# Transformer chain on one core: slots of all steps placed anew, first batch's start reordered, Newton's steps for 1/norm moved from VectorE to GpSimdE

## The chip, the cores and the metric

The kernel runs on one core of a Trainium2 chip. The core has TensorE (matmuls; PE in the profile, its weight loads are PEld), VectorE (DVE), ScalarE (ACT), GpSimdE (POOL) and SyncE (SP), which here issues all the DMAs. The engines run beside each other, each its own program in order, and meet through semaphores. The metric is the time of one execution on the device, in microseconds (us); lower is better.

## The reference

The input x has 16 batches of 512 tokens with 128 channels. Four blocks are added to it in turn, each on the layernorm of x:

```
x = x + attn_a(layernorm(x))      # latent attention, 16 heads, causal, softmax
x = x + ffn(layernorm(x))         # sigmoid(xr W_r) * (relu(xk W_k)^2 W_v), x mixed with the token before
x = x + attn_b(layernorm(x))      # q and k normalised to length 1 per head, causal, softmax of 8 * q.k
x = x + ffn(layernorm(x))
```

The step of attn_b that the change touches is

```
q, k = (t / max(sqrt(sum(t * t)), 1e-12) for t in (q, k))     # per token and head, 8 channels
```

## The kernel before

**The work of a batch.** All 512 tokens of a batch are worked on at once, as 4 tiles of 128. A batch passes these stages (methods of `Stages`, one version for each engine):

- `prepare_front`: layernorm "1" (statistics on DVE, `rstd` on POOL, `xn` on DVE, transposed by PE, evicted as `xnT` by ACT), then `project`: queries and keys by two matmuls (L611), each result split in three bf16 parts, part 0 by ACT (L874), part 1 by DVE (L1045, L1048), part 2 by POOL (L1296). SP writes the parts to DRAM (`scratch`) in the three pieces of `STACK` (L1433).
- `restack`: SP reads them back with the products of parts stacked along the contraction (`stack_qa`, `stack_ka`, L1453).
- `row_maxima` and `max_rows`: all scores of attention a once for their maxima (PE L636, DVE L1074, in two groups of pairs), which are turned and written into rows of `stack_qa` by four small DMAs (`mturned`, L1472).
- `attend a`: scores again (L705), `exp` on ACT (L923, `prob`), weighted sums (L722, `acc`); `middle_front`: residual and the first feed-forward block.
- `middle_back`: layernorm "3", `project_qk` (L777), sums of squares `ssum` (DVE L1167), `rsqrt`, `turn_qk` (L1199 multiplies by `rnorm`, PE L795 transposes, split as above), then `restack` and `attend b`; `finish`: output projection and the second feed-forward block, `store`.

**rsqrt.** 1/sqrt(`ssum`) for 128 x 128 numbers is made on DVE from an integer seed (two operations, L1178 and L1180) by three steps of Newton, each three operations on DVE (L1184, L1187, L1189), eleven in all. The POOL version of `rsqrt` is empty.

**What sets the order.** `halves` lists the 32 attention halves (a and b of each batch, the a half three batches ahead); each has 36 slots. `stages_of` gives each yield of a stage a slot, by the table `PLANS` relative to its half: a class `None` for most batches, and classes for batches 0, 1, 2, -2 and -1. `turns` sorts all yields by slot and runs them through the generators of each engine, so the table sets the order in which every engine's instructions stand. `Places` runs the same order first and gives out the PSUM banks (`pool0` to `pool3`), each free when its former user's reader is done. `setup` is a stage too, with three yields: identity and constants; the five products of weights for the first projection (PE L581, L585; ACT L841, L838) with POOL's `ones_rows` and masks; the other products and POOL's clearing of `vals`. PE leaves such a yield only when all its products have been evicted.

**In the steady part** DVE's maxima for the next batch, ACT's exponentials and PE's matmuls of two halves are interleaved. Three two-bank tiles of PSUM are shared by the maxima (freed by DVE) and the scores (freed by ACT).

Of the kernel before, what the change touches and what calls it, by code (L numbers as in the profile page):

```python
# [6 lines left out]
ALU, ACT, AX = mybir.AluOpType, mybir.ActivationFunctionType, mybir.AxisListType  # L7
# [21 lines left out]
SLOTS = 36  # L29
# [19 lines left out]
        "half_norm_b": [27],  # L49
        "finish": [34, 35, 39, 42, 45, 49, 54, 54, 56, 57, 63, 68],  # L50
    },
    0: {
        "load": [-159],
        "prepare_front": [-138, -125, -114, -113, -109],
        "restack_a": [-73, -68],
        "row_maxima0": [-63.8, -62.2, -53.8, -50.8, -45.2, -45.2, -42.8, -42.2, -36],
        "max_rows0": [-24, -23],
        "row_maxima1": [-31, -30.2, -20, -16.2, -14.8, -10.8, -6.2, -1.8, -1.8],
        "max_rows1": [1, 6],
        "values_a": [-38, -32],  # L60
        "half_norm": [19],
        "middle_front": [39, 41, 47, 51, 54, 57, 61, 63, 69, 71],
        "restack_b": [95, 98],
        "middle_back": [72, 75, 78, 81, 81, 82, 83, 86, 89, 90, 92],
        "values_b": [-42, -30],
        "half_norm_b": [27],
# [4 lines left out]
        "prepare_front": [-62, -59, -53, -48, -46],  # L71
        "restack_a": [-42, -37],
        "row_maxima0": [-29, -28, -28, -27, -26, -25, -22, -18, -18],
        "max_rows0": [-17, -15],
        "row_maxima1": [-14, -14, -10, -8, -7, -6, -5, -5, -4],
        "max_rows1": [0, 6],
        "values_a": [-47, -38],
        "half_norm": [20],
        "middle_front": [37, 38, 44, 48, 54, 59, 60, 61, 68, 69],
        "restack_b": [102, 129],  # L80
        "middle_back": [82, 90, 94, 98, 100, 103, 106, 107, 116, 118, 122],
        "values_b": [-30, -28],
        "half_norm_b": [34],
        "finish": [42, 44, 44, 47, 51, 56, 56, 60, 61, 63, 70, 73],
    },
    2: {
        "load": [-94],
        "prepare_front": [-66, -58, -54, -52, -50],
        "restack_a": [-66, -56],
        "row_maxima0": [-26.2, -26.2, -23.2, -23.2, -20, -20, -20, -17, -16.2],  # L90
        "max_rows0": [-16, -13],
        "row_maxima1": [-12, -10, -10, -9, -8, -7, -5, -4, -3],
        "max_rows1": [-1, 4],
        "values_a": [-38, -19],
        "half_norm": [18],
        "middle_front": [38, 40, 44, 48, 54, 59, 61, 63, 69, 71],
        "restack_b": [115, 118],
        "middle_back": [72, 79, 85, 90, 90, 91, 94, 97, 107, 109, 113],
        "values_b": [-35, -35],
# [4 lines left out]
        "load": [-158],  # L104
        "prepare_front": [-117, -107, -102, -99, -91],
        "restack_a": [-92, -90],
        "row_maxima0": [-60, -58, -55, -51, -47, -46, -44, -36, -36],
        "max_rows0": [-31, -21],
# [3 lines left out]
        "half_norm": [20],  # L112
        "middle_front": [36, 38, 41, 48, 54, 57, 60, 63, 69, 73],
        "restack_b": [130, 140],
        "middle_back": [76, 79, 85, 90, 91, 93, 94, 97, 107, 108, 108],
        "values_b": [-43, -32],
        "half_norm_b": [25],
        "finish": [36, 37, 38, 41, 45, 49, 50, 57, 58, 58, 66, 67],
    },
    -1: {  # L120
        "load": [-158],
        "prepare_front": [-114, -107, -99, -96, -91],
        "restack_a": [-73, -73],
        "row_maxima0": [-60, -58, -56, -51, -46, -44, -44, -36, -36],
# [1438 lines left out]
```

## Time and profile before

| | us |
|---|---|
| median of 3 runs | 1134.62 (1133.15 to 1136.98) |
| the profiled execution's own time | 1134.93 |
| its span | 1133.1 |
| PE busy | 958.4 (85%) |
| DVE busy | 880.5 (78%) |
| ACT busy | 769.5 (68%) |
| POOL busy | 281.6 (25%) |

The span is what the trace covers; the execution's own time is 1.8 us longer. From 400 us to 827 us the program repeats with a period of about 60.9 us, one batch each. Before it stand the start and the three batches of lead, behind it the end, where stages run out of work to overlap with.

### The profile page before, as it was taken

The numbers are of one execution on the slowest core, as the hardware profiler recorded it, in microseconds if no ns is written. First come the engines' busy times: TensorE is split into PE (matmuls) and PEld (weight loads), VectorE is DVE, ScalarE is ACT, GpSimd is POOL, SyncE is SP. The second block draws the span as 40 slices with busy tenths as digits, with TensorE's granted clock in tenths as the row PEclk, the third lists the DMA queues.
The fourth block names the chain that finished last, engine by engine and source line by source line (L and its number), as shares of the span: only waits on it lengthen the run. The fifth ranks groups of instructions, "written<-read, shape, count | busy, mean of one in ns | idle before, by whom it ended". The sixth has DMA issues, their size and how long they took to land.

```text
span 1133.1 us, 36161 instructions
## 1 busy us (share of the span) xinstructions
PE 958.4 (85%) x15409; PEld 524.0 (46%) x15409; DVE 880.5 (78%) x2112; ACT 769.5 (68%) x1042; POOL 281.6 (25%) x264
## 2 busy tenths in 40 slices
PE   3469787778888989999999989999989889899694
PEld 1224344344454545545454545455555445455353
DVE  3658677688869889898989898989989797875632
ACT  2036456566766777778887877787777777788672
POOL 5110131222312223132313222232313132222212
PEclk9979798899989999999999999999999999999897
DMA  3353153244642708072534536271908254324140
GB/s 103 52 123 90 36 124 83 50 105 117 141 102 66 181 17 216 25 195 53 155 83 108 139 90 156 67 180 39 207 13 196 48 137 94 88 40 122 47 77 19
DMA packets 86145, 112.86 MB, mean 100 GB/s; under 512 B 13152, under 2 KB 79840, under 8 KB 79840
## 3 DMA queue, kind: packets, MB, share of 16 engines
q1 hardware_dynamic: 85984, 110.55, 40.7%
q8 instruction: 121, 1.98, 0.8%
q14 instruction: 40, 0.33, 0.1%
HBM read 55.22 MB, written 54.53 MB: 97 GB/s over the span
## 4 chain that ended last, share of the span: by engine, by line
PE 39%; DVE 30%; ACT 12%; DMA 7%; issue 7%; SPq 2%; POOL 2%; POOLq 0%; DVEq 0%; ACTq 0%
PE acc L722 12%; DVE rowmax L1074 12%; ACT prob L923 8%; PE pool L705 6%; PE pool L636 4%; DMA stack_ka<-scratch_ka 3%; DVE xn L1032 3%; PE pool L755 2%; PE pool L749 2%; PE pool L777 2%; DVE stats L1020 2%; PE pool L601 2%; PE pool L652 2%; DMA stack_qb<-scratch_qb 2%; PE pool L674 2%
## 5 line engine op out<-in xcount | busy, mean ns | idle before, releaser
L923 ACT ACTIVATE prob<-pool 128x1024 f32<-128x1024 f32 x576 | 565.4, 1029 | 156.8 <-PE pool L652 152.3
L1074 DVE TENSOR_REDUCE rowmax<-pool 128x2 f32<-128x1024 f32 (+7 forms) x480 | 357.8, 792 | 100.7 <-PE pool L652 97.6
L722 PE MATMUL acc<-prob,vals_a 128*32 128x512 f32 (+7 forms) x2048 | 170.8, 429 | 0.2 <-ACT prob L923 0.2
L722 PE MATMUL acc<-prob,vals_b 128*32 128x512 f32 (+7 forms) x2048 | 164.1, 422 | 1.2 <-DVE turned_b L1109 0.7
L636 PE MATMUL pool<-stack_ka,stack_qa 48*64 48x512 bf16 (+7 forms) x2048 | 118.7, 306 | 53.9 <-issue 17.7
L705 PE MATMUL pool<-stack_qa,stack_ka 51*64 51x512 bf16 (+7 forms) x2048 | 113.1, 300 | 31.5 <-DVE rowmax L1074 18.2
L705 PE MATMUL pool<-stack_qb,stack_kb 48*64 48x512 bf16 (+7 forms) x2048 | 112.9, 297 | 24.2 <-ACT prob L923 9.6
L652 PE MATMUL pool<-mask_t,ident_b 64*64 64x128 bf16 (+1 forms) x2304 | 130.0, 215 | 0.0
L636 PEld LDWEIGHTS pool<-stack_ka,stack_qa 48*64 48x64 bf16 x2048 | 43.1, 109 | 146.3 <-ACT prob L923 57.6
L1284 POOL TENSOR_TENSOR rstd<-mv,minus_half 128x4 f32<-128x4 f32 x64 | 65.3, 1021 | 154.0 <-DVE mv L1027 154.0
L1296 POOL TENSOR_TENSOR parts_q<-rest_q,parts_q 128x512 bf16<-128x512 f32 x32 | 37.0, 1157 | 196.2 <-DVE parts_q L1048 196.1
L705 PEld LDWEIGHTS pool<-stack_qa,stack_ka 51*64 51x64 bf16 x2048 | 42.8, 108 | 85.1 <-issue 25.4
L705 PEld LDWEIGHTS pool<-stack_qb,stack_kb 48*64 48x64 bf16 x2048 | 42.8, 107 | 81.4 <-issue 35.0
L722 PEld LDWEIGHTS acc<-prob,vals_b 128*32 128x32 f32 x2048 | 50.8, 110 | 61.9 <-issue 31.7
L652 PEld LDWEIGHTS pool<-mask_t,ident_b 64*64 64x64 bf16 x2304 | 68.9, 109 | 19.9 <-issue 2.6
L1347 POOL TENSOR_TENSOR ffn_act<-ffn_act 128x512 f32<-128x512 f32 x32 | 33.5, 1047 | 178.1 <-ACT ffn_act L947 178.1
L722 PEld LDWEIGHTS acc<-prob,vals_a 128*32 128x32 f32 x2048 | 49.3, 110 | 58.0 <-issue 36.6
L652 PE MATMUL pool<-mask,ident_b 64*64 64x128 bf16 (+1 forms) x1152 | 66.4, 219 | 3.4 <-issue 3.4
L601 PE MATMUL pool<-ident,xn 128*128 128x128 f32 x256 | 43.3, 302 | 25.3 <-DVE xn L1032 23.7
L864 ACT ACTIVATE xnT<-pool 128x512 f32<-128x512 f32 x64 | 37.6, 607 | 30.8 <-PE pool L601 30.6
L1296 POOL TENSOR_TENSOR parts_k<-rest_k,parts_k 128x512 bf16<-128x512 f32 x32 | 37.6, 1174 | 71.5 <-DVE parts_k L1048 71.5
L1342 POOL TENSOR_TENSOR ffn_diff<-xnT 128x512 f32<-128x512 f32 x32 | 33.1, 1036 | 66.5 <-ACT xnT L864 66.5
(129 smaller groups left out, 1390.5 us busy)
## 6 DMA issues: line engine op xcount, KB each, us to landing
stack_qa<-scratch_qa SPq DMA_DIRECT2D x32, 384.0 KB, 7.1
stack_ka<-scratch_ka SPq DMA_DIRECT2D x32, 384.0 KB, 7.7
stack_kb<-scratch_kb SPq DMA_DIRECT2D x32, 384.0 KB, 5.6
stack_qb<-scratch_qb SPq DMA_DIRECT2D x32, 384.0 KB, 6.8
scratch_qa<-parts_q SPq DMA_DIRECT2D x16, 384.0 KB, 3.5
scratch_ka<-parts_k SPq DMA_DIRECT2D x16, 384.0 KB, 6.0
scratch_qb<-parts_q SPq DMA_DIRECT2D x16, 384.0 KB, 2.6
scratch_kb<-parts_k SPq DMA_DIRECT2D x16, 384.0 KB, 2.6
```

The costliest lines, as they stand in the source:

```text
L601: made_ = eng.transpose(ps[:, P * k:P * k + P], xn[n][:, k, :], ident[:, :])
L636: eng.matmul(ps[half:half + BLK, k, at:at + w], queries[rows, pair, BLK * blk:w], keys[rows, pair, 0:w], start=i_piece < 2, stop=False)
L652: last = self.eng.matmul(to, ident_b[rows, rows], m[rows, 0:len(own), :], start=False, stop=True)
L705: eng.matmul(ps[half:half + BLK, k, at:at + w], keys[rows, pair, BLK * blk:BLK * blk + BLK], queries[rows, pair, BLK * blk:T], start=i_pie ...
L722: last = eng.matmul(acc[32 * j:32 * j + 32, BLK * blk:T], vals[a][:, blk, GROUP * g + j, :], prob[n % NPROB][:, k, at:at + T - BLK * blk], ...
L864: eng.activation(xnT_of(n, b)[:, 1:T + 1], ps[:, :], ACT.Copy).then_inc(S["xnT" + n], 1)
L923: eng.activation(prob[n % NPROB][:, :, :], place["unit", n][0][:, :, :], ACT.Exp, scale=scale).then_inc(S["exped"], 1)
L1032: last = eng.tensor_scalar(o[:, k, :], x_of(src, b)[:, k, :], m[:, k, 0:1], r[:, k:k + 1], ALU.subtract, ALU.mult)
L1074: last = eng.tensor_reduce(to, of, axis=AX.X, op=ALU.max)
L1284: eng.tensor_tensor(rstd[n][:, :], mv[n][:, :, 1], minus_half[:, 0:1].to_broadcast([P, NT]), ALU.pow).then_inc(S["rstd" + n], 1)
L1296: eng.tensor_tensor(parts[n][:, 2, :], rest[n][:, :], parts[n][:, 1, :], ALU.subtract).then_inc(S[f"part2_{n}{a}"], 1)
L1347: eng.tensor_tensor(ffn["act"][:, :], ffn["act"][:, :], ffn["act"][:, :], ALU.mult).then_inc(S["act" + n], 1)
```

## The change

1. `PLANS`: numbers of all six classes differ, mostly by 1 to 10 slots. Among them `restack_b` of class `None` goes from 102, 126 to 97, 135.
2. Start: the second yield of `setup` now stands behind yield 1 of `prepare_front` (the `xn` step) and no longer behind yield 2 (the transposition), and POOL's clearing of `stack_ka` waits for `xn1` and no longer for `rstd1`.
3. `rsqrt`: DVE keeps the two seed operations; POOL does the three steps of Newton in four operations each with at most two operands, twelve in all.
4. SP's `split`: each write of parts waits for the last part that it holds, not for part 2, and the pieces of k are written in the opposite order (so the smallest, part 0 alone, goes first).
5. `end_a` for batches that have none before them is -140 and not -76.

```diff
     None: {
-        "load": [-137],
-        "prepare_front": [-117, -108, -99, -96, -90],
-        "restack_a": [-96, -79],
+        "load": [-139],
+        "prepare_front": [-117, -106, -99, -96, -90],
+        "restack_a": [-113, -91],
...
-        "restack_b": [102, 126],
-        "middle_back": [73, 80, 85, 90, 90, 93, 94, 98, 107, 109, 113],
+        "restack_b": [97, 135],
+        "middle_back": [73, 78, 85, 90, 90, 91, 94, 98, 107, 109, 113],
...
-            end_a = {k: SLOTS * (half_of["a", b - k] + 1) if b >= k else -76 for k in (1, 2)}
+            end_a = {k: SLOTS * (half_of["a", b - k] + 1) if b >= k else -140 for k in (1, 2)}
...
-            steps += [(slot + 0.1, setup) for slot in (load[0], front[2], front[4])]
+            steps += [(slot + 0.1, setup) for slot in (load[0], front[1], front[4])]
...
             def rsqrt(self, b):                                   # DVE
...
-                for k in range(3):
-                    q.wait_ge(S["newton"], n + 3 * k + 2)
-                    eng.scalar_tensor_tensor(step_r[:, :], rnorm[:, :], -0.5, rnorm[:, :], ALU.mult,
-                                             ALU.mult).then_inc(S["newton"], 1)
-                    q.wait_ge(S["newton"], n + 3 * k + 3)
-                    eng.tensor_tensor(step_r[:, :], step_r[:, :], ssum[:, :], ALU.mult).then_inc(S["newton"], 1)
-                    q.wait_ge(S["newton"], n + 3 * k + 4)
-                    eng.scalar_tensor_tensor(rnorm[:, :], step_r[:, :], 1.5, rnorm[:, :], ALU.add,
-                                             ALU.mult).then_inc(S["newton"], 1)
+                for _ in range(3):
                     yield
...
-                q.wait_ge(S["rstd1"], 1)
+                q.wait_ge(S["xn1"], 1)
                 self.ones_rows(0)
...
             def rsqrt(self, b):                                   # POOL
-                yield
-                yield
-                yield
+
+                eng, q = self.eng, self.q
+                for k in range(3):
+                    n = 14 * b + 4 * k + 2
+                    q.wait_ge(S["newton"], n)
+                    eng.tensor_tensor(step_r[:, :], rnorm[:, :], rnorm[:, :], ALU.mult).then_inc(S["newton"], 1)
+                    q.wait_ge(S["newton"], n + 1)
+                    eng.tensor_tensor(step_r[:, :], step_r[:, :], ssum[:, :], ALU.mult).then_inc(S["newton"], 1)
+                    q.wait_ge(S["newton"], n + 2)
+                    eng.tensor_scalar(step_r[:, :], step_r[:, :], -0.5, 1.5, ALU.mult, ALU.add).then_inc(S["newton"], 1)
+                    q.wait_ge(S["newton"], n + 3)
+                    eng.tensor_tensor(rnorm[:, :], rnorm[:, :], step_r[:, :], ALU.mult).then_inc(S["newton"], 1)
+                    yield
...
-                for first, *chosen in STACK:
+                for first, *chosen in STACK if n == "q" else STACK[::-1]:
...
-                    q.wait_ge(S[f"part2_{n}{a}"], b + 1)
+                    q.wait_ge(S[f"part{c[-1]}_{n}{a}"], b + 1)
```

**PE at the start.** The program's first matmuls, before:

```order
L601 MATMUL pool<-ident,xn 128x128 x4
L581 MATMUL pool<-ident,raw_uq 64x128
L585 MATMUL pool<-raw_dq,T_uq 128x128
L585 MATMUL pool<-T_uq,raw_dq 128x128
L585 MATMUL pool<-M_qT,raw_uk 64x128
L585 MATMUL pool<-k_effT,raw_dkv 128x128
L611 MATMUL pool<-xnT,M_q 128x512
```

and now:

```order
L581 MATMUL pool<-ident,raw_uq 64x128
L585 MATMUL pool<-raw_dq,T_uq 128x128
L585 MATMUL pool<-T_uq,raw_dq 128x128
L585 MATMUL pool<-M_qT,raw_uk 64x128
L585 MATMUL pool<-k_effT,raw_dkv 128x128
L601 MATMUL pool<-ident,xn 128x128 x4
L611 MATMUL pool<-xnT,M_q 128x512
```

The products of weights (`raw_*` are the loaded weights) stood behind the transposition of the first batch's `xn`; they stand ahead of it now.

**DVE around Newton's steps in the steady part.** Before, from the sums of squares to the multiplication `qk<-raw,rnorm` (the last rows are those just ahead of it):

```order
L1167 TENSOR_REDUCE ssum<-qk 128x64 x2
L1178 TENSOR_SCALAR ssum<-ssum 128x128
L1180 TENSOR_SCALAR rnorm<-ssum 128x128
L1184 SCALAR_TENSOR_TENSOR step_r<-rnorm 128x128
L1187 TENSOR_TENSOR step_r<-step_r,ssum 128x128
L1189 SCALAR_TENSOR_TENSOR rnorm<-step_r,rnorm 128x128
L1074 TENSOR_REDUCE rowmax<-pool 128x2 x2
L1184 SCALAR_TENSOR_TENSOR step_r<-rnorm 128x128
L1187 TENSOR_TENSOR step_r<-step_r,ssum 128x128
L1189 SCALAR_TENSOR_TENSOR rnorm<-step_r,rnorm 128x128
L1074 TENSOR_REDUCE rowmax<-pool 128x2 x2
```

and now:

```order
L1167 TENSOR_REDUCE ssum<-qk 128x64 x2
L1178 TENSOR_SCALAR ssum<-ssum 128x128
L1180 TENSOR_SCALAR rnorm<-ssum 128x128
L1074 TENSOR_REDUCE rowmax<-pool 128x2 x6
L1157 SCALAR_TENSOR_TENSOR ffn_prod<-ffn_gate,pool 128x512
L1020 BN_STATS stats<-x_in 128x6 x4
L1024 BN_AGGR mv<-stats 128x2 x4
L1027 TENSOR_SCALAR mv<-mv 128x4
L1074 TENSOR_REDUCE rowmax<-pool 128x2 x2
L1125 RECIPROCAL rden_a<-pool 128x32
L1132 TENSOR_TENSOR y_a<-pool,rden_a 128x4x64
L1191 TENSOR_TENSOR qk<-raw,rnorm 128x512 x2
```

Nine operations are gone between the seed and `qk`; all other operations between them were there before, in the same order.

**POOL at the same place, now** (before, only `ffn_act` stood between `ffn_diff` and `x_out`):

```order
L1334 TENSOR_TENSOR ffn_diff<-xnT 128x512
L1363 TENSOR_TENSOR step_r<-rnorm 128x128
L1365 TENSOR_TENSOR step_r<-step_r,ssum 128x128
L1367 TENSOR_SCALAR step_r<-step_r 128x128
L1369 TENSOR_TENSOR rnorm<-rnorm,step_r 128x128
L1339 TENSOR_TENSOR ffn_act<-ffn_act 128x512
L1363 TENSOR_TENSOR step_r<-rnorm 128x128
L1365 TENSOR_TENSOR step_r<-step_r,ssum 128x128
```

Behind these rows come the other six operations of Newton, then `x_out` (L1349) and the next `rstd`.

**SP in the steady part.** The writes to and reads from `scratch` of one period, before:

```order
L1433 DMA scratch_qa<-parts_q 128x512
L1453 DMA stack_qb<-scratch_qb 48x4096 x2
L1433 DMA scratch_ka<-parts_k 128x3x512
L1433 DMA scratch_ka<-parts_k 128x2x512
L1433 DMA scratch_ka<-parts_k 128x512
L1453 DMA stack_qa<-scratch_qa 48x4096 x2
L1453 DMA stack_ka<-scratch_ka 48x4096 x2
L1472 DMA stack_qa<-mturned 3x16x64 x4
```

and now:

```order
L1435 DMA scratch_qa<-parts_q 128x512
L1435 DMA scratch_ka<-parts_k 128x512
L1435 DMA scratch_ka<-parts_k 128x2x512
L1435 DMA scratch_ka<-parts_k 128x3x512
L1455 DMA stack_qa<-scratch_qa 48x4096 x2
L1455 DMA stack_ka<-scratch_ka 48x4096 x2
L1455 DMA stack_qb<-scratch_qb 48x4096 x2
L1474 DMA stack_qa<-mturned 3x16x64 x4
```

The read of `stack_qb` moved from ahead of `scratch_ka` to behind `stack_ka`, and the pieces of k go out smallest first.

## Rows read from the trace of the kernel before

**Rows 1.** Busy time by stretch: us, PE, PEld, DVE, ACT, POOL, PEclk, DMA share, GB/s.

```profile
522.55:583.40 60.85, 56.46 (x967) 31.15 (x963) 54.44 (x132) 47.74 (x64) 16.67 (x15) 1.00 0.45 115
891.00:954.50 63.50, 57.23 (x967) 31.36 (x963) 55.09 (x133) 48.02 (x65) 16.98 (x15) 1.00 0.45 106
```

**Rows 2.** PE's waits, 340 to 827 us: total us, times, longest.

```profile
PE pool L705 <- ACT prob L923: 11.8, 28, 0.8
PE pool L705 <- DVE rowmax L1074: 6.4, 15, 1.1
PE pool L636 <- DVE rest_k L1045: 4.7, 8, 0.7
PE pool L674 <- DVE rowmax L1074: 2.0, 8, 0.5
```

**Rows 3.** Chain that ended last, 522.6 to 583.45 us: start, us, what.

```profile
528.80 1.29 DVE rowmax L1074 x2
530.09 0.21 DVE step_r L1184
```

**Rows 4.** Timeline of PE, one steady period; in brackets the idle time before.

```profile
532.20 0.41 PE L705 MATMUL pool<-stack_qa,stack_ka 51*64 51x320 bf16 x8 [0.60 <-DVE rowmax L1074]
```

**Rows 5.** Timeline of DVE, the same period.

```profile
527.19 0.23 DVE L1180 TENSOR_SCALAR rnorm<-ssum 128x128 int32<-128x128 int32 x1
527.45 0.29 DVE L1184 SCALAR_TENSOR_TENSOR step_r<-rnorm 128x128 f32<-128x128 f32 x1
...
538.06 1.28 DVE L1199 TENSOR_TENSOR qk<-raw,rnorm 128x512 f32<-128x512 f32 x2
```

**Rows 6.** Timeline of POOL, the same period.

```profile
528.22 1.07 POOL L1347 TENSOR_TENSOR ffn_act<-ffn_act 128x512 f32<-128x512 f32 x1 [7.60 <-ACT ffn_act L947]
```

**Rows 7.** Timeline of the start, all engines.

```profile
1.42 0.20 POOL L1235 MEMSET ident_b<- 128x128 bf16 x1
1.77 0.29 POOL L1237 TENSOR_SCALAR_AFFINE_SELECT ident_b<-ident_b 128x128 bf16<-128x128 bf16 x1
...
3.03 0.50 SPq L1399 DMA_DIRECT2D raw_dkv<-in_L_attn_a_W_dkv  x1
...
6.51 3.86 DVE L1032 TENSOR_SCALAR xn<-x_in,mv,rstd 128x128 f32<-128x128 f32 x4 [1.22 <-POOL rstd L1284]
6.54 3.69 POOL L1274 MEMSET stack_ka<- 32x2048 f32 x2
...
11.40 0.42 PE L581 MATMUL pool<-ident,raw_uq 128*64 128x128 f32 x1
...
11.65 0.60 ACT L864 ACTIVATE xnT<-pool 128x512 f32<-128x512 f32 x1 [9.63 <-PE pool L601]
...
15.49 0.47 ACT L838 ACTIVATE M_k<-pool 128x32 f32<-128x32 f32 x4 [0.88 <-PE pool L585]
...
16.00 2.07 PE L611 MATMUL pool<-xnT,M_q 128*128 128x512 f32 x2 [0.56 <-ACT M_k L838]
...
22.93 2.17 SPq L1433 DMA_DIRECT2D scratch_ka<-parts_k  x3
...
37.71 0.64 PE L636 MATMUL pool<-stack_ka,stack_qa 48*64 48x512 bf16 x4 [14.40 <-issue]
```

**Rows 8.** DMAs, 0 to 45 us: KB each, median us from issue to landing.

```profile
raw_dkv<-in_L_attn_a_W_dkv SPq DMA_DIRECT2D x1, 32.0 KB, 2.1
```

**Rows 9.** Line L1032, whole span: duration ns min/median/max, first and last start.

```profile
L1032 DVE TENSOR_SCALAR xn<-x_in,mv,rstd x64: 333/342/1905, 6.5 to 913.3; 128x128 f32<-128x128 f32 x64
```

**Rows 10.** PE's waits, 827 to 1133 us.

```profile
PE pool L636 <- DMA stack_ka<-scratch_ka: 2.4, 2, 1.5
```

**Rows 11.** Timeline of DVE in the last batch.

```profile
1063.14 0.23 DVE L1180 TENSOR_SCALAR rnorm<-ssum 128x128 int32<-128x128 int32 x1
...
1066.34 1.29 DVE L1199 TENSOR_TENSOR qk<-raw,rnorm 128x512 f32<-128x512 f32 x2
```

**Rows 12.** Timeline of PE in the last batch.

```profile
1089.40 0.41 PE L705 MATMUL pool<-stack_qb,stack_kb 48*64 48x512 bf16 x4 [1.31 <-DMA stack_qb<-scratch_qb]
```

More of the change, by code:

```diff
@@ new lines @@
+        "finish": [34, 36, 39, 42, 46, 49, 54, 54, 56, 57, 63, 69],
+    },
+    0: {
+        "load": [-158],
+        "prepare_front": [-134, -123, -110, -105, -105],
+        "restack_a": [-74, -67],
+        "row_maxima0": [-63, -63, -53, -50, -46, -45.2, -45.2, -42.2, -37.8],
+        "max_rows0": [-30, -21],
+        "row_maxima1": [-33.2, -31.8, -23.2, -17.8, -17.8, -13.2, -9.2, -1.8, -1.8],
+        "max_rows1": [0, 3],
+        "values_a": [-30, -18],
+        "half_norm": [19],
+        "middle_front": [39, 41, 47, 51, 54, 58, 61, 63, 69, 71],
+        "restack_b": [97, 100],
+        "middle_back": [72, 75, 78, 81, 81, 82, 83, 86, 89, 90, 90],
+        "values_b": [-38, -24],
+        "half_norm_b": [28],
@@ L103 @@
     -2: {
[L104 to L108, printed above, removed]
+        "load": [-149],
+        "prepare_front": [-116, -107, -102, -99, -91],
+        "restack_a": [-100, -100],
+        "row_maxima0": [-60, -58, -55, -51, -47, -46, -46, -36, -36],
+        "max_rows0": [-25, -11],
         "row_maxima1": [-32, -32, -25, -19, -17, -14, -10, -7, -6],
@@ L111 @@
         "values_a": [-35, -35],
[L112 removed]
+        "half_norm": [18],
         "middle_front": [36, 38, 41, 48, 54, 57, 60, 63, 69, 73],
[L114 removed]
+        "restack_b": [135, 140],
         "middle_back": [76, 79, 85, 90, 91, 93, 94, 97, 107, 108, 108],
[L116 to L118 removed]
+        "values_b": [-51, -42],
+        "half_norm_b": [20],
+        "finish": [36, 37, 38, 41, 45, 49, 50, 57, 58, 65, 66, 67],
     },
     -1: {
[L121 removed]
+        "load": [-168],
         "prepare_front": [-114, -107, -99, -96, -91],
[L123 removed]
+        "restack_a": [-79, -74],
         "row_maxima0": [-60, -58, -56, -51, -46, -44, -44, -36, -36],
[L125 removed]
+        "max_rows0": [-33, -28],
         "row_maxima1": [-32, -32, -25, -23.2, -17, -14, -10, -7, -6],
[L127 to L135 removed]
+        "max_rows1": [-2, 6],
+        "values_a": [-42, -40],
+        "half_norm": [27],
+        "middle_front": [41, 44, 45, 45, 54, 57, 57, 63, 69, 71],
+        "restack_b": [95, 97],
+        "middle_back": [73, 76, 78, 80, 80, 84, 84, 85, 86, 87, 87],
+        "values_b": [-47, -43],
+        "half_norm_b": [20],
+        "finish": [35, 36, 38, 40, 40, 42, 45, 46, 49, 49, 54, 64],
     },
@@ L1175, in rsqrt @@
                 eng, q = self.eng, self.q
-                n = 11 * b
+                n = 14 * b
                 q.wait_ge(S["norms2"], 2 * (b + 1))
```

80 lines of the change are left out of this document (28 added, 52 removed).

## The prediction

> **What bounds the kernel now.** I read the busy time by stretch first. In a steady period of 60.85 us PE is busy 56.46, DVE 54.44, ACT 47.74 and POOL 16.67, at a granted clock of 1.00 [rows 1]. So PE is near its bound, DVE is close behind and POOL has room. At the start, until PE's first scores at 37.71 [rows 7], PE stood still for the last 14.4 us, so there a chain of latencies counts.
>
> Second, who makes PE wait. Over the eight periods from 340 to 827 us the DVE releases account for 6.4 + 4.7 + 2.0 = 13.1 us, 1.6 a period, and ACT's exponentials for 11.8 [rows 2]. Third, the chain of waits in one period: from 528.80 it runs on DVE, and Newton's steps stand in it between the maxima [rows 3]. The timeline of PE shows what that costs: 0.60 us before 532.20, released by a maximum [rows 4], and the wait of the values' matmuls at the end of this run, 2.0 us in eight times [rows 2], 0.25 a period. The 0.6 us a period by `rest_k` comes later, behind pauses of DVE, so what DVE saves here doesn't reach it directly.
>
> **Term 1, the start.** First the `xn` step. Four operations took 3.86 us [rows 7] where the median of one is 342 ns, the longest being 1905 [rows 9]; POOL's clearing of `stack_ka` ran for the same time, 6.54 to 10.23. With POOL waiting for `xn1`, `xn` takes about 1.4 and ends at 7.9 instead of 10.37. That is no longer the latest, since the products of weights now stand ahead of the transposition. The last weight is issued by 3.53 and lands 2.1 later [rows 7, 8], so the products can begin at 5.6. From the first product (11.40) to `M_k` evicted (15.96) it took 4.56 [rows 7], hence 10.2; the transposition and its eviction come behind it, 1.9 us (from `xn`'s end at 10.37 to the eviction's at 12.25), hence 12.1 for the first projection, against 16.00: 3.9 us sooner. POOL's clearing and masks (5.9 us, behind 7.9) end at 13.8, ahead of its first part 2 at about 16; they are hidden.
>
> Then SP. All of k's three writes waited for part 2 and were issued from 22.93 to 25.10 [rows 7]. Now only the last one is left at that point, about 0.5 us of issue: 1.6 us sooner. But the last is now the largest piece, which may land some 0.4 later. Together 3.9 + 1.6 - 0.4 = 5.1 us by which PE's first scores (37.71) come sooner. Bounds 3.5 and 6.5 (if the landing of the large piece eats the split, or the weights land earlier than I count).
>
> **Term 2, Newton off DVE.** Nine operations of 0.29 us with their gaps, 0.94 a step (0.29 for each [rows 5], 0.03 between), make 2.8 us less DVE work in each batch. Two of the three steps, 1.88 us, lay in DVE's unbroken run from 528.80 on [rows 3]. PE can get back what it waited: 0.60 + 0.25 = 0.85 directly [rows 2, 4], not more than 1.6 on the average by releases of DVE [rows 2], with ACT's waits, which hang on the same PSUM tiles, at most the 1.88. Bounds 0 and 1.88; I take 0.9, near the direct row. Batches: eight steady ones, two stretched ones behind them, three before 340 us: 13 x 0.9 = 11.7 us.
>
> The cover. POOL's price for a 128x128 operation isn't in the trace. A clearing of 128 columns takes 0.20, one of 2048 half of 3.69 [rows 7], which gives 0.09 fixed; with 512 columns of two operands at 1.07 [rows 6], 128 come to 0.09 + 0.98 / 4 = 0.33. Bounds: 0.20 (the clearing) and 1.07 (no scaling at all). Between dependent operations of POOL lie 0.15 [1.42 + 0.20 to 1.77, rows 7]. So 0.48 each and 5.8 us for twelve. Started at 527.45 behind the seed, with `ffn_act` (1.07) among them, they end at 534.3. DVE reaches `qk` at 538.06 - 2.8 = 535.2: covered with 0.9 us to spare, and up to 538.06 nothing is worse than before, which is a pitch of 0.80 us. Queued behind them on POOL are `x_out`, whose sum only feeds a store, and the next `rstd` (its `xn` now stands behind `y_a`, some 3 us later in DVE's order). `ffn_act` slips by about 1 us; it was done at 529.29 [rows 6], and PE's matmuls on it stand behind the scores that began at 532.20 [rows 4].
>
> Rule against the change: the Trainium skill, GPSIMD Engine Reference, "Engine selection", says elementwise work belongs on VectorE, GpSimd being about twice as slow with two inputs. Its figure of 2.6 cycles at 1.2 GHz for each element would make 0.28 us of 128 columns, an estimate from that page, and twelve with my gaps 5.2 us. What the rule leaves out is which of the two engines is late, and here only DVE is.
>
> **Term 3, the late restacks.** Twice behind 827 us PE waits for the read of `stack_ka`, 2.4 us in all [rows 10]. The read of `stack_qb`, 768 KB, stood ahead of it on SP and in the queue; it now stands behind. `stack_qb` itself is needed only by the next b half. I take the whole 2.4; bounds 0 and 5 (the second of these periods is 63.5 us long against 60.85 [rows 1], so more may hang on it).
>
> **Term 4, the last batch.** Here nothing covers Newton: seed done at 1063.37, `qk` at 1066.34, 2.97 us [rows 11]. Now 5.8: 2.8 us later. The writes of q and k get back 1.6 as at the start. PE waits for this read at 1089.40 [rows 12], so all of the difference shows: +1.2. Bounds -0.5 and +8 (a pitch of 0.26, or of 1.2).
>
> **Term 5, the other slots and PSUM tiles.** In the steady part DVE's and PE's order differ by a few neighbours. Between 38 and 80 us batch 1's statistics go behind `mparts` (later by some 1 us) while its restack gains what the split writes give. I put 0; bounds -3 and +3. The changed `end_a` moves nothing, for no slot is bound by either number.
>
> **Sum**, against the profiled execution's own 1134.93, which is 0.3 above the median of the runs: 1134.9 - 5.1 - 11.7 - 2.4 + 1.2 = 1116.9, say 1117 us.
>
> **Rivals.**
> - *Hidden relief.* PE is 93% busy and ACT's waits (11.8) are as long as DVE's; if the saved DVE time only turns into DVE's idle time, term 2 is 0: 1134.9 - 5.1 - 2.4 + 1.2 = 1128.6. For it: PE has only 4.4 us of idle time in a period. Against: the waits that make the 0.85 lie in and at the end of DVE's unbroken run.
> - *More than the direct waits.* The maxima free PSUM sooner, ACT's waits shrink with them, and new slots use it: 1.88 x 13 = 24.4 instead of 11.7, so 1104.2. For it: the chain holds the two steps whole [rows 3].
> - *The shared port.* POOL's clearing stretched an `xn` operation from 342 to 1905 ns [rows 7, 9]. Twelve small POOL operations meet some ten DVE operations that read SBUF (`ffn_prod`, statistics, aggregates); each waiting half of 0.33 us makes 1.7 of the saved 2.8. A third of term 2 is left, 4.2 us: 1124.4. The Trainium skill, SBUF — State Buffer, "SBUF: two separate sides", has the pair of ports as an exclusive lock for a whole instruction, and the trace's stretched `xn` agrees; against a large price stands that the maxima read PSUM.
> - *Slower: POOL too slow.* If a 128-column operation costs as much as one of 512 columns (the 4-column `rstd` takes 1.02 too, though by a power), the pitch is 1.2 us. Newton ends at 527.45 + 14.4 + 1.07 = 542.9, `qk` is 4.9 us later than before and DVE's maxima queue behind it: 15 x 4.9 = 73, the last batch 14.4 - 3.0 = 11 more: 1134.9 - 5.1 - 2.4 + 73 + 11 - 1.6 = 1210. It decides from a pitch of 0.80 on, and eats all other gains from about 0.85. Against it: the clearings scale with their columns.
> - *The start is given back* before 80 us, because batch 1's chain is later and waits for the same DMAs: 1117 + 5.1 = 1122.
>
> **How the numbers follow.** Forecast 0.52 (own range 1110 to 1125); hidden relief 0.17; more 0.13; port 0.08; POOL too slow 0.05; start given back 0.05. Outside a range of 1105 to 1129 lie the lower half of "more", the slow POOL and the upper edge of "hidden", some 0.17. A difference under 0.3%, 3.4 us, can't be told from none here: 1131.2 is the bound. All of "slow" and 0.01 of the last are slower, 0.06. "Same" gets 0.07, 0.03 of "hidden" and the upper edges of the others. Faster 0.87.
>
> **What would show it.** PE's first scores at 32.5 (31 to 34). POOL's 128-column operations 0.3 to 0.4 us, their pitch near 0.5, no DVE idle time before `qk` in the steady part. Period of 60.0 (59.0 to 60.3), PE busy unchanged at 56.5, its waits for `rowmax` smaller by 0.85 and those for ACT not larger. No wait for `stack_ka` behind 827. In the last batch seed to `qk` about 5.8. Wrong it would be if the period stays at 60.8, or if `qk` waits for POOL.

## The result, and the profile after

The changed kernel takes 1121.68 us, the median of 4 runs (1116.43 to 1124.93), against 1133.88 of the kernel before, measured beside it. The ratio is 0.9892 with a 95% interval from 0.9849 to 0.9936: 12 us faster. I had said 1117, in a range from 1105 to 1129. The number held, but the terms behind it did not: two were wrong by 10 us and more, in opposite directions, so that 1117 came as near as it did by luck.

The profiled execution took 1124.93 us, its span is 1123.1. Busy: PE 964.3, DVE 847.9 (880.5 before), ACT 769.6, POOL 359.0 (281.6). By stretch, one steady period and one late one (columns as in [rows 1]; the late one runs from the store of one batch to the store of the next):

```profile
516.67:577.66 60.99, 56.57 (x964) 31.49 (x963) 53.03 (x123) 47.82 (x65) 21.39 (x27) 1.00 0.49 115
882.96:949.92 66.96, 57.88 (x970) 32.54 (x966) 50.34 (x122) 47.25 (x64) 21.67 (x27) 0.97 0.45 101
```

The second row of [rows 1] is not cut at the stores. Between the same two stores the kernel before has:

```profile
904.91:967.92 63.01, 57.41 (x975) 31.69 (x974) 54.48 (x132) 47.88 (x65) 16.96 (x15) 1.00 0.45 107
```

The steady period is 60.99 where it was 60.85: nothing gained, though DVE has less to do. The late one has grown from 63.01 to 66.96. PE's waits in the steady part, 331.53 to 820.01 us (total us, times, longest), answering to [rows 2]:

```profile
PE pool L705 <- DVE rowmax L1074: 9.5, 17, 0.9
PE pool L705 <- ACT prob L923: 7.9, 20, 0.8
PE pool L661 <- DVE mparts L1092: 4.2, 7, 0.6
PE pool L636 <- ACT prob L923: 2.1, 7, 0.3
```

ACT's waits have shrunk (11.8 in [rows 2], now 7.9), DVE's maxima have grown into the largest item, 9.5. That is not what I had forecast (smaller by 0.85 a period). The timeline of the start, answering to [rows 7]:

```profile
5.23 0.40 PE L581 MATMUL pool<-ident,raw_uq 128*64 128x128 f32 x1 [5.23 <-DMA raw_dkv<-in_L_attn_a_W_dkv]
...
6.48 1.12 DVE L1032 TENSOR_SCALAR xn<-x_in,mv,rstd 128x128 f32<-128x128 f32 x4 [1.22 <-POOL rstd L1276]
...
7.65 3.65 POOL L1266 MEMSET stack_ka<- 32x2048 f32 x2 [1.21 <-DVE xn L1032]
...
9.54 1.11 PE L601 MATMUL pool<-ident,xn 128*128 128x128 f32 x4 [0.56 <-ACT M_k L838]
...
11.34 2.07 PE L611 MATMUL pool<-xnT,M_q 128*128 128x512 f32 x2 [0.69 <-ACT xnT L864]
...
16.94 1.70 SPq L1435 DMA_DIRECT2D scratch_ka<-parts_k  x3
...
31.33 0.64 PE L636 MATMUL pool<-stack_ka,stack_qa 48*64 48x512 bf16 x4 [13.59 <-issue]
```

`xn` takes 1.12 instead of 3.86, the products begin at 5.23, and PE's first scores come at 31.33 instead of 37.71. The last batch on DVE, answering to [rows 11], with the first step of Newton on POOL between (POOL's rows for the other two steps are left out):

```profile
1049.16 0.23 DVE L1180 TENSOR_SCALAR rnorm<-ssum 128x128 int32<-128x128 int32 x1
1049.46 0.40 POOL L1363 TENSOR_TENSOR step_r<-rnorm 128x128 f32<-128x128 f32 x1 [5.00 <-DVE rnorm L1180]
1049.94 0.46 POOL L1365 TENSOR_TENSOR step_r<-step_r,ssum 128x128 f32<-128x128 f32 x1
1050.48 0.30 POOL L1367 TENSOR_SCALAR step_r<-step_r 128x128 f32<-128x128 f32 x1
1050.87 0.45 POOL L1369 TENSOR_TENSOR rnorm<-rnorm,step_r 128x128 f32<-128x128 f32 x1
...
1055.21 1.29 DVE L1191 TENSOR_TENSOR qk<-raw,rnorm 128x512 f32<-128x512 f32 x2 [5.83 <-POOL rnorm L1369]
```

A step takes 1.94 us from its first operation to the next step's first (1049.46 to 1051.40), the twelve operations 5.8. The wait of [rows 12] is gone. That of [rows 10], PE's for `stack_ka` behind 820 us, has grown instead:

```profile
929.96 0.64 PE L636 MATMUL pool<-stack_ka,stack_qa 48*64 48x512 bf16 x4 [4.44 <-DMA stack_ka<-scratch_ka]
```

### The profile page after: what moved, and what is told of

The parts are those of the page before. It is cut to its first block, busy times and chain, and to the rows that moved or that the text cites. A ratio compares the mean times of both kernels' runs of the same rounds, so it can differ in the third digit from the quotient of the medians.

```text
span 1123.1 us, 36212 instructions
## 1 busy us (share of the span) xinstructions
PE 964.3 (86%) x15409; PEld 530.1 (47%) x15409; DVE 847.9 (75%) x1968; ACT 769.6 (69%) x1042; POOL 359.0 (32%) x456
## 4 chain that ended last, share of the span: by engine, by line
PE 47%; DVE 30%; ACT 9%; issue 6%; DMA 4%; POOL 3%; SPq 1%; DVEq 0%; POOLq 0%; ACTq 0%
PE acc L722 15%; DVE rowmax L1074 12%; PE pool L705 8%; ACT prob L923 5%; DVE xn L1032 4%; PE pool L636 4%; PE pool L601 3%; PE pool L749 3%; PE pool L755 3%; PE pool L763 2%; PE pool L777 2%; PE pool L652 2%; DMA stack_ka<-scratch_ka 2%; DVE stats L1020 2%; DVE qk L1191 2%
## 5 line engine op out<-in xcount | busy, mean ns | idle before, releaser
L705 PE MATMUL pool<-stack_qb,stack_kb 48*64 48x512 bf16 (+7 forms) x2048 | 116.5, 301 | 26.8 <-DVE rowmax L1074 11.2
```

The lines of the kernel that those rows point to most:

```text
L705: eng.matmul(ps[half:half + BLK, k, at:at + w], keys[rows, pair, BLK * blk:BLK * blk + BLK], queries[rows, pair, BLK * blk:T], start=i_pie ...
```

## The experiments

Twelve kernels, each timed against the kernel before in five rounds. An execution of one and the same kernel varies by about 0.5% to either side (the kernel before from 1126 to 1139), so verdicts come from the ratios, and single traces serve for waits and for stages of constant length. To divide a trace I use DVE's seed of each batch (`rnorm<-ssum`, L1180). It lies ahead of Newton's steps; the stores do not serve, since `x_out` can queue on POOL behind Newton's steps without anybody waiting for it. Here is every kernel with its ratio, and the length of its stages in us (seed of batch 0, from there to those of batches 5, 11 and 15, and on to the end of the span):

| kernel | ratio (95%) | to 0 | 0-5 | 5-11 | 11-15 | to end |
|---|---|---|---|---|---|---|
| before | 1 | 172.8 | 293.5 | 365.4 | 231.4 | 70.0 |
| start alone | 0.9937 (0.9909 to 0.9965) | 165.6 | 289.0 | 365.6 | 230.8 | 70.8 |
| Newton alone | 1.0031 (1.0006 to 1.0055) | 171.6 | 290.6 | 366.2 | 233.8 | 74.2 |
| split alone | 0.9878 (0.9851 to 0.9905) | 165.3 | 286.3 | 365.0 | 232.3 | 69.9 |
| slots alone | 1.0019 (0.9990 to 1.0047) | 170.9 | 284.1 | 367.6 | 229.9 | 71.2 |
| start + split | 0.9900 (0.9875 to 0.9924) | 162.2 | 286.1 | 365.6 | 231.9 | 69.8 |
| all but Newton | 0.9868 (0.9832 to 0.9903) | 164.2 | 281.0 | 367.0 | 233.8 | 70.1 |
| all but slots | 0.9930 (0.9907 to 0.9953) | 161.6 | 290.3 | 365.3 | 230.8 | 73.6 |
| all but split | 0.9984 (0.9958 to 1.0010) | 162.9 | 280.8 | 367.6 | 237.1 | 74.3 |
| all (the change) | 0.9892 (0.9849 to 0.9936) | 161.7 | 283.2 | 366.7 | 237.7 | 73.9 |
| all, Newton on DVE in batches 14, 15 | 0.9819 (0.9790 to 0.9848) | 160.6 | 280.1 | 366.3 | 233.9 | 70.2 |
| split where counted | 0.9974 (0.9948 to 1.0000) | 168.7 | 293.5 | 365.6 | 231.7 | 69.7 |
| split, waits only | 0.9974 (0.9951 to 0.9997) | 167.2 | 290.7 | 365.0 | 234.5 | 70.1 |
| split, order only | 1.0014 (0.9984 to 1.0044) | 172.9 | 288.5 | 366.2 | 235.5 | 69.8 |

Of these stages 5-11 and "to end" are constant enough to compare two traces; 0-5 and 11-15 are not: "before" and "split, order only" differ there by 5.0 and 4.1 us, in opposite directions, at a ratio of 1.0014. Some traces come from an execution far from its kernel's median: "slots alone" 8 us under it, "all but split" 7, "start alone" 3.5, and "all" 3.3 over it.

**The four parts alone.** The start:

```diff
-            steps += [(slot + 0.1, setup) for slot in (load[0], front[2], front[4])]
+            steps += [(slot + 0.1, setup) for slot in (load[0], front[1], front[4])]
-                q.wait_ge(S["rstd1"], 1)
+                q.wait_ge(S["xn1"], 1)
                 self.ones_rows(0)
```

> The kernel before with the reordered start alone (setup's second yield behind the xn step, POOL's ones_rows behind xn1). Theory A (each term lies in its own stage; PE's first scores come sooner by some 4 us, and what is gained there is kept because the 33 to 340 us stretch is a chain behind it): first scores at about 33.5 instead of 37.7, every store from the first on 3 to 4 us sooner, time 0.3% less (1130). Rival B (the start is taken up again by the maxima stage of batches 0 to 2, where DVE is the bound): first scores sooner by 4, first store by less than 1, time the same as before.

Measured 1126.91 us, 0.63% less: about 7 us. First scores at 32.92, 4.8 sooner, and kept: theory A, with somewhat more than its 3 to 4 us. Rival B is out. The two edits, the place of the products and the wait for `xn1`, were not tried apart.

Newton's steps on POOL, as in the change, all else as before.

> The kernel before with Newton's steps on GpSimdE alone, old slots, old start. Theory A (where PE is nearly full, VectorE's saved 2.8 us per batch turn into its idle time; where VectorE is the bound, ahead of 340 us, they count; in the last batch they cost 2.9 us): store times at 340 us 3 to 8 us sooner, period from 340 to 827 still 60.8, end +3; in sum 0 to 5 us faster. Rival B (my term of 0.9 us a batch was right, and in the full change the new slots took it back): period 60.0, time 8 to 10 us less, 1124. Rival C (the old slots put qk too early for GpSimdE): qk waits, time longer than before.

Measured 1135.9, 0.31% more: slower than before, outside what theory A allowed. The seeds of the steady part still follow each other by 60.85 to 60.86 us in four of the six periods between batches 5 and 11, against 60.83 to 60.85 in five of them before. What became of DVE's saved time stands in DVE's waits, 353.03 to 840.79 us of the kernel before:

```profile
DVE rowmax L1074 <- PE pool L652: 34.2, 48, 2.4
```

and 350.56 to 837.41 us with Newton on POOL (no wait by `ffn_prod` was listed before):

```profile
DVE rowmax L1074 <- PE pool L652: 46.8, 55, 2.9
DVE ffn_prod L1157 <- PE pool L763: 3.7, 7, 0.5
```

That is 16.3 us more waiting for PE in eight periods, 2.0 a period, which is what DVE's busy time fell by (54.44 in [rows 1], 52.50 in the row below). The steady period of the kernel with Newton on POOL by stretch, and PE's waits by the maxima from 341 to 828 us:

```profile
532.06:592.92 60.86, 56.78 (x966) 31.20 (x962) 52.50 (x124) 47.74 (x65) 21.43 (x27) 1.00 0.47 116
```

```profile
PE pool L705 <- DVE rowmax L1074: 4.4, 15, 0.4
PE pool L674 <- DVE rowmax L1074: 2.6, 7, 0.5
```

So DVE waited for PE before already, 4.3 us a period, and I had not looked at that row. PE's own waits by `rowmax` at the scores did shrink, from 6.4 in fifteen times [rows 2] to 4.4 in as many, but those at the values' matmuls grew from 2.0 to 2.6: together 0.2 us a period less, and the period stayed. Rival B is out, and so is rival C: `qk` waits for POOL in three batches only, by 2.1 us in the first (where seed to `qk` is 6.11, before it was 6.24), by 0.5 in batch 14 and by 5.9 in batch 15. At the end the cost is plain: 4.2 us more from the last seed to the end of the span.

Of these 4.2 only 2.9 are Newton's longer chain. PE waits for the last `qk` for 5.83 us instead of 2.94, and the same eight matmuls that follow take 1.97 us instead of 1.09. Before:

```profile
1067.69 1.09 PE L795 MATMUL pool<-ident,qk 128*128 128x128 f32 x8 [2.94 <-DVE qk L1199]
```

and with Newton on POOL:

```profile
1069.55 1.97 PE L795 MATMUL pool<-ident,qk 128*128 128x128 f32 x8 [5.83 <-DVE qk L1191]
```

The granted clock while they ran was 1.00 before and is 0.50 now (the lower of the two levels, 1.2 GHz); in the idle time ahead of them it was 1.00 before (1065.00 to 1067.69) and 0.70 now (1063.70 to 1069.50). Over the whole last stage PE is busy 48.45 us for 614 matmuls that took 47.07, which is about the rest.

SP's writes:

```diff
-                for first, *chosen in STACK:
+                for first, *chosen in STACK if n == "q" else STACK[::-1]:
...
-                    q.wait_ge(S[f"part2_{n}{a}"], b + 1)
+                    q.wait_ge(S[f"part{c[-1]}_{n}{a}"], b + 1)
```

> The kernel before with SP's split writes alone (each waits for the last part that it holds, k's smallest piece first). Theory A: first scores 1 to 1.6 us sooner, 0 to 1 us less for the whole. In the last batch the restack lands about 1.5 us sooner and the end comes by that much sooner: 2 to 3 us less in all. Rival B (the wait at the head of SP's queue only moves; the large piece goes last and lands as late as before): first scores and last batch within 0.5 us of before, time the same.

Measured 1119.99, 1.22% less. Both theories were far off: these two lines alone are worth 14 us, as much as the whole change. First scores 1.8 us sooner, the last stage no shorter (70.0, now 69.9), since PE, which no longer waits 1.3 us for `stack_qb` there, waits 1.1 us for `vals_b` from ACT. PE's waits where restacked operands come in, in the kernel before: batch 1's, batch 2's, the first b half's, and one near the second b half's read (two of them without a releaser, "issue"):

```profile
79.17 0.64 PE L636 MATMUL pool<-stack_ka,stack_qa 48*64 48x512 bf16 x4 [6.23 <-DMA stack_ka<-scratch_ka]
119.49 0.41 PE L636 MATMUL pool<-stack_ka,stack_qa 48*64 48x512 bf16 x4 [3.01 <-issue]
205.12 0.64 PE L705 MATMUL pool<-stack_qb,stack_kb 48*64 48x512 bf16 x4 [5.88 <-DMA stack_qb<-scratch_qb]
312.70 0.32 PE L652 MATMUL pool<-mask,ident_b 64*64 64x128 bf16 x4 [3.42 <-issue]
```

and with the split writes:

```profile
76.00 0.64 PE L636 MATMUL pool<-stack_ka,stack_qa 48*64 48x512 bf16 x4 [4.04 <-DMA stack_ka<-scratch_ka]
113.81 0.41 PE L636 MATMUL pool<-stack_ka,stack_qa 48*64 48x512 bf16 x4 [0.86 <-issue]
194.76 0.64 PE L705 MATMUL pool<-stack_qb,stack_kb 48*64 48x512 bf16 x4 [3.09 <-issue]
299.13 0.25 PE L652 MATMUL pool<-mask,ident_b 64*64 64x128 bf16 x4 [0.43 <-issue]
```

They are 2.2, 2.1, 2.8 and 3.0 us shorter; with the first scores' 1.8 that makes 11.9 us. What the second and the fourth waited for the trace doesn't name; that it was the restacks is read from where they stand. The cause shows on SP. In the restack of batch 1's b half k's part 2 is done at 293.91 in the kernel before, and the read of `stack_kb` is issued at 299.31, 5.4 us later:

```profile
293.98 1.56 SPq L1433 DMA_DIRECT2D scratch_kb<-parts_k  x3
299.31 0.79 SPq L1453 DMA_DIRECT2D stack_kb<-scratch_kb  x2
```

With the split it is 283.33 and 286.51, 3.2 us, because the writes begin ahead of part 2:

```profile
280.73 2.99 SPq L1433 DMA_DIRECT2D scratch_kb<-parts_k  x3
286.51 0.79 SPq L1453 DMA_DIRECT2D stack_kb<-scratch_kb  x2
```

The table of slots.

> The kernel before with the new table of slots alone. Theory A (the table is what gains between the start and the second store, about 9 to 12 us of the 15 found there, and what loses 8 to 12 us behind 883 us; steady part unchanged): second store 9 to 12 us sooner, end within 3 us of before. Rival B (the table was placed for Newton on GpSimdE and is worth nothing or costs time without it): second store within 3 us of before. Rival C (the slots of class None are what keeps the period at 60.8 in the full change): period here longer than 60.8, 61 to 62.

Measured 1133.48, the same as before. This trace is of an execution of 1125.55 us, 8 less than the median, so its stages don't add up to the ratio. What holds over all kernels is that stage 0-5 is shorter with the new slots (280.1 to 284.1 us in five kernels) than with the old ones (286.1 to 293.5 in nine), and 5-11 a little longer (366.3 to 367.6 against 365.0 to 366.2). Rival C is half right: the even 60.84 turns into periods from 60.2 to 63.4.

**Three parts at a time.**

> The kernel before with the reordered start and SP's split writes, old slots, Newton on VectorE. The parts alone gave -6.5 us (start) and -13.4 us (split). Theory A (the parts add up, each takes waits of its own in the first 340 us): 1113.5 us, both stores at 282 and 353 us of before some 18 to 22 us sooner. Rival B (both shorten the same chain up to batch 1's and 2's restacks, so they overlap): 1118 to 1120 us, no better than the split alone. Either way about 1.0 to 1.5 us sooner than the split at PE's first scores plus the start's 4.8.

Measured 1119.39, no better than the split alone: rival B by the time. By the traces it isn't settled: the two together are 4.7 us ahead of the split at the first scores (31.20), 3.1 at the seed of batch 0 and 3.1 at the end of the span, and the runs' spread is as large as that. Where the start's gain goes when the split is there stays open.

> The full change but Newton's steps on VectorE as before. Newton alone cost 3.5 us (ratio 1.0031). Theory A (it costs 3 us in the last batch, where nothing covers it, and gives nothing elsewhere, whatever the slots): 1118.5 us against 1121.7 of the full change, last batch's seed to qk 3.2 instead of 5.8. Rival B (the new slots need the relieved VectorE): slower than the full change, 1123 or more, waits for rowmax grow.

Measured 1116.27, theory A: Newton on VectorE is faster, by 0.24% between the ratios, with intervals that overlap. Together with the part alone (1.0031) and with 0.9930 against 0.9900 for the old slots it is the third comparison with the same sign and size: Newton on POOL costs about 3 us in sum. Only the interval of the first leaves out 1.

> The full change but the old table of slots. Alone the table did nothing (ratio 1.0019). Theory A (the parts add up): 1119 to 1121 us, like the full change, though its stores lie elsewhere: less gain ahead of 340 us and less loss behind 883 us. Rival B (the new table costs time once the split has taken the restacks' waits away, as the stack_qb read behind stack_ka does in the last batches): 1115 to 1117 us.

Measured 1123.91, more than either theory expected: without the new slots the change is slower by 0.38% between the ratios, which are not apart for certain (0.9930 and 0.9892). The pair without Newton on POOL says the same (0.9900 and 0.9868). In this pair of traces the new slots make stage 0-5 7.1 us shorter and stage 11-15 6.9 longer. Of the latter the wait for `stack_ka` is a part. Behind 815 us it is 2.4 us in the kernel before, and in the three kernels with the split and the old slots 0.3, 0.2 and none (this one); in the three with the split and the new slots it is 2.4, 3.7 and 4.4. So the split removes this wait, and the new slots bring it back.

> The full change but SP's writes as before. Theory A (the split is worth 13 us in the full change as it is alone): 1132 to 1134 us, waits for stack_qb (5.9 us) and stack_ka (6.2 us) back in the first 340 us. Rival B (the new slots move restack_a of class 0 and the start far enough ahead that the split is worth only the part at the first scores): 1124 to 1127 us.

Measured 1131.26: theory A, the split is worth 0.92% in the full change. The wait for `stack_qb` (3.5 us in the first 340) is back; that for `stack_ka` is 6.5, but it is 5.4 in the change too, so it had hardly gone.

**Where Newton's cost lies, and a faster version.** In every kernel with Newton on POOL, the last stage is 73.6 to 74.3 instead of 69.7 to 71.2, and from the seed of batch 14 to that of batch 15 it is 46.1 to 46.9 instead of 44.6 to 44.9. So in the full change I gave VectorE the steps of these two batches back:

```diff
+DVE_FROM = 14
...
-                for _ in range(3):
+                for k in range(3):
+                    if b >= DVE_FROM:
...
                     yield
...
                 for k in range(3):                                # POOL
+                    if b >= DVE_FROM:
+                        yield
+                        continue
```

> The full change, with Newton's steps on VectorE again for the last two batches (14 and 15) alone. Theory A (GpSimdE's steps lose 3.5 to 4 us in each of the last two store periods, where qk waits for them by 1.7 and 5.8 us, and cost nothing before): last two periods 56.5 and 61.6 instead of 60.4 and 65.6, 1114 to 1116 us, 6 to 7 us less than the full change. Rival B (GpSimdE's steps cost a little in every batch, through late qk or a shared port): 1118 to 1120 us, slower than the variant with all steps on VectorE (1116.3). Rival C (they gain some 4 us ahead of batch 14): 1111 to 1113 us, the fastest of all.

Measured 1112.81 us, 0.9819 (0.9790 to 0.9848): the fastest of all and 8 us under the full change by the ratios (the intervals don't overlap, though their ends touch within 0.0001). The number is that of rival C, the mechanism shown that of theory A. The trace, seed and `qk` of batches 14 and 15 (the added lines shift the numbers):

```profile
995.95 0.23 DVE L1181 TENSOR_SCALAR rnorm<-ssum 128x128 int32<-128x128 int32 x1
1001.11 1.93 DVE L1201 TENSOR_TENSOR qk<-raw,rnorm 128x512 f32<-128x512 f32 x2
1040.84 0.23 DVE L1181 TENSOR_SCALAR rnorm<-ssum 128x128 int32<-128x128 int32 x1
1044.03 1.29 DVE L1201 TENSOR_TENSOR qk<-raw,rnorm 128x512 f32<-128x512 f32 x2
```

From seed to `qk` 5.16 and 3.19, where the change needs 6.88 and 6.05. The last stage is 3.8 shorter, 44.89 between the seeds instead of 46.90: 5.8 us that the traces show, of which PE's lower clock in these stages is a part (in the change the eight matmuls on `qk` take 1.78 and 1.97 us, here 1.09 both times). For the other 2 to 3 us I have no cause. Against the kernel with all steps on VectorE (1116.27) the intervals overlap, so whether POOL's steps gain in the other fourteen batches (rival C) stays open.

**Where the split's gain lies.** Only in the two restacks that my prediction counted:

```diff
+                early = (b, a) in ((0, "a"), (15, "b"))
-                for first, *chosen in STACK:
+                for first, *chosen in STACK[::-1] if early and n == "k" else STACK:
...
-                    q.wait_ge(S[f"part2_{n}{a}"], b + 1)
+                    q.wait_ge(S[f"part{c[-1] if early else 2}_{n}{a}"], b + 1)
```

> The kernel before with SP's split writes only where my prediction counted them: the restack a of batch 0 and the restack b of the last batch. All others as before. Theory A (the 13.4 us of the split come mostly from restacks that I left out, those of batches 1 to 3 and the first b restacks, each of which PE waits for until 340 us): 1 to 3 us less than before, waits for stack_ka (6.2) and stack_qb (5.9) back. Rival B (they come from the two counted places, by a chain that multiplies them): 10 us less or more.

Measured 1131.36, 0.26% less: theory A. Waits for `stack_ka` 5.2 and `stack_qb` 6.0 are there. Some 11 of the 14 us come from the restacks that I left out.

The new waits, with k's pieces in the old order:

```diff
-                    q.wait_ge(S[f"part2_{n}{a}"], b + 1)
+                    q.wait_ge(S[f"part{c[-1]}_{n}{a}"], b + 1)
```

> The kernel before with the new waits of SP's writes but k's pieces in the old order (so k's largest piece goes first and still holds the queue until part 2; only q's pieces go out early). Theory A (q's writes going out under the splitting of k frees SP's queue and the DMA engines by the time that k's parts are ready): q's part of the gain, a third to a half, 5 to 7 us less than before. Rival B (the queue's head is k's part 2 in any case, and only k's early pieces count): the same as before within 1.5 us. Rival C (q alone gives all of it, and k's reversed order nothing): 12 us less or more.

Measured 1130.99, 0.26% less, some 3 us: between rival B's 1.5 and theory A's 5 to 7. The read of `stack_kb` still follows part 2 by 5.5 us (286.30 to 291.83).

The new order, with the old waits:

```diff
-                for first, *chosen in STACK:
+                for first, *chosen in STACK if n == "q" else STACK[::-1]:
```

> The kernel before with k's pieces written smallest first, all of them still waiting for part 2 (the order half of the split; the waits half alone gave 0.9974, both together 0.9878). Theory A (what counts is that two of k's writes leave SP while GpSimdE makes part 2, which needs the new wait and the new order together): ratio 0.998 to 1.002, SP's three writes still follow part 2 and the read of stack_kb is issued some 5.4 us behind part 2 as before (3.2 with the split). Rival B (the order itself does it, since the largest write goes last and the small ones don't queue behind it): ratio 0.99, read issued 3 to 4 us behind part 2. Theory A's own check: waits for stack_qb (5.9) and stack_ka (6.2) stay.

Measured 1133.86, the same as before: theory A. The read of `stack_kb` follows part 2 by 5.1 us (291.72 to 296.83), nearly as before. So neither line does it alone; k's small pieces must stand ahead of the large one and be allowed to go before part 2. PE's two waits stay:

```profile
79.37 0.64 PE L636 MATMUL pool<-stack_ka,stack_qa 48*64 48x512 bf16 x4 [6.55 <-DMA stack_ka<-scratch_ka]
...
204.58 0.64 PE L705 MATMUL pool<-stack_qb,stack_kb 48*64 48x512 bf16 x4 [5.26 <-DMA stack_qb<-scratch_qb]
```

## Why the prediction was right in the sum and wrong in its terms

I had written that I would be wrong if the period stays at 60.8, or if `qk` waits for POOL. By these signs the explanation failed, for the first came true, and the second in the first batch and in the last two; only the sum came out, and that is luck: alone, the four parts measure about -7 (start), -14 (split), +3.5 (Newton) and +2 (slots, not to be told from none), where I had added up -5.1 for the start with the split, -11.7 for Newton, -2.4 for late restacks and +1.2 for the last batch.

- **Term 1, the start (-5.1): right in mechanism and nearly in size.** First scores moved by 6.4, within the bound of 6.5. `xn` ended at 7.60 (I said 7.9), the first projection began at 11.34 (12.1), since the products could start at 5.23. Of the 6.4, the start alone gives 4.8 (I said 3.9) and the split 1.8 (1.2). Whether the start is worth anything in the whole time once the split is there stays open.
- **The split was mis-sized, the largest error: 14 us against 2.8.** The step that failed: I read the wait for SP's writes at two places only, the first scores and the last batch. The same 2 us stand in each restack that PE waits for, and PE's waits ahead of 340 us name them: `stack_ka` 6.2, `stack_qb` 5.9 and "issue" 17.4 (of which 14.4 ahead of the first scores). I had taken the waits from 340 us on, where restacks are ahead of their use. Of the two places that I counted, the last batch gave nothing: its wait of 1.31 [rows 12] goes, but one for ACT's `vals_b` comes in its place, and the last stage stays at 69.9.
- **Term 2, Newton off DVE (-11.7): wrong, 0 in the steady part.** My step "PE can get back what it waited" failed. PE's direct waits by DVE's maxima shrank by 0.2 us a period and not by 0.85, and in the full change they grew. DVE itself waited for PE 4.3 us a period in the same stretch, and its saved 2.0 us went there. So DVE is not the late one; which chain holds the period at 60.85 no run shows. This is the mechanism of the rival "hidden relief", to which I gave 0.17; its 1128.6 was wrong too, for it kept the split's small price. The cover was right in the steady part, where `qk` doesn't wait for POOL. Of the other rivals, "more" and "POOL too slow" are out (period 60.85, pitch 0.48); of "the shared port" the steady part shows 0.4 us a period.
- **Term 4, the last batch (+1.2): the sign right, too small, and a second batch forgotten.** The twelve operations took 5.8 us as I said. The last stage grew by about 4, of which 2.9 is the longer chain and the rest PE at the lower clock behind its longer wait, a cost that my sum didn't have; and batch 14, which I had not looked at, costs 1.5 to 2 more. The bounds that I gave (-0.5 and +8) don't follow from the pitches beside them, which make -1.5 and +9.8; the measured cost lies inside either. I had priced the cover at one steady period and carried it to all thirteen batches; the batches at the end have less of it.
- **Term 3, the late restacks (-2.4): wrong.** The wait is 4.44, in one batch. I read SP's new order in a steady period; in the late batch the read of `stack_qb` still stands ahead, and all three behind the four small writes of `mturned`:

```profile
909.65 2.96 SPq L1474 DMA_DIRECT2D stack_qa<-mturned  x4
912.65 0.90 SPq L1455 DMA_DIRECT2D stack_qb<-scratch_qb  x2
913.65 2.30 SPq L1455 DMA_DIRECT2D stack_qa<-scratch_qa  x2
915.99 0.89 SPq L1455 DMA_DIRECT2D stack_ka<-scratch_ka  x2
```

The read of `stack_ka` then takes 13.37 us to land. The place behind `stack_qb` is not the whole cause, for with the old slots `stack_qb` stands ahead there too and PE doesn't wait. I had credited the slots with what the split does: with the old slots the split alone takes this wait from 2.4 to 0.3.

- **Term 5, the slots (0): small in sum, as I said, but by two large effects.** The ratios give +0.2% alone and -0.4% in the full change, neither clear of noise. The stages show some 7 us gained ahead of the seed of batch 5; the loss behind it is seen in part, 1 to 2 us up to the seed of batch 11 and, in the kernels with the split, 1.5 to 7 from there to batch 15 (233.8 to 237.7 against 230.8 to 232.3).
- **The price on POOL.** I estimated 0.33 for an operation and 0.48 for the pitch. The pitch is 0.48, by two errors that cancel. Over the whole span, count, busy us and mean ns of one:

```profile
L1365 POOL TENSOR_TENSOR step_r<-step_r,ssum 128x128 f32<-128x128 f32 x48 | 22.5, 470 | 3.8
...
L1363 POOL TENSOR_TENSOR step_r<-rnorm 128x128 f32<-128x128 f32 x48 | 19.2, 399 | 92.4 <-DVE rnorm L1180 91.0
L1367 POOL TENSOR_SCALAR step_r<-step_r 128x128 f32<-128x128 f32 x48 | 15.0, 312 | 4.2
```

Operations take 0.31 to 0.47, the gap between dependent ones is 0.08 instead of 0.15. The Trainium skill, GPSIMD Engine Reference, "Elementwise — side-by-side cycle accounting", has 2.6 cycles an element for two inputs, from which I estimated 0.28; the measured 0.47 is longer, so at this size the figure leaves out a fixed part. Two inputs of 512 columns (`x_out`) take 1.27 in the same trace and two of 128 take 0.46 in the median: 2.1 ns a column and 0.19 fixed, an estimate from these two. Its rule in "Engine selection", elementwise work on VectorE, held here in sum (about 3 us lost), and for the latency in the last two batches, which the rule doesn't speak of.

## What to carry to other kernels

Before you credit an engine with time that it saves, read the waits of that engine too: if it waits in the same period for the engine that you want to speed up, the saving becomes more waiting. When an edit changes a step that runs in every batch, list every place where the bound engine waits for that step, in each stage, and not only the first and the last. Moving work to a slower engine under cover needs the cover checked in every batch: at the end of the program it is gone, and keeping the old way for the last batches can be worth more than the move. A longer wait of TensorE can cost more than its length: here the granted clock had fallen to 0.50 when it went on.

## What the runs showed that I had not expected

- A relief of 2.0 us a period on an engine that was busy 54.4 of 60.85 us changed the period by nothing (60.85 and 60.86).
- A DMA's wait and its place in the queue work only together: 0.26% for the waits, 0 for the order, 1.22% for both.
- Newton's steps shift POOL's other work, and where it falls beside certain operations of DVE, these run longer. With Newton alone on POOL, one `mv<-mv` in each of two neighbouring steady periods takes 0.64 us where it took 0.22 (`x_out` now runs on POOL beside it, 530.76 to 532.04), and in batch 14 of the full change `qk` takes 2.34 for two operations that take 1.28 in most batches, while `x_out` runs on POOL:

```profile
1009.06 1.27 POOL L1349 TENSOR_TENSOR x_out<-x_b,ffn_prod 128x512 f32<-128x512 f32 x1
1009.14 2.34 DVE L1191 TENSOR_TENSOR qk<-raw,rnorm 128x512 f32<-128x512 f32 x2 [1.74 <-POOL rnorm L1369]
```

  The price is small in the steady part: over eight periods all of `mv<-mv` takes 8.8 us instead of 5.7, and the nine operations that are gone had taken 22.0.
